# Four scatters issued at the end of the routing, and two products of the first unit made on VectorE

## The reference

```
xn = layernorm(x)
s  = mamba(xn)             # two directions, each with 16 states:
       dt = softplus(x_dbl[..., :64] @ Wdt.T + bdt)
       dBu = dt * B[n] * x ;  deltaA = exp(dt * A[n])        # n = 0..15
       carry = deltaA_t * carry + dBu_t ;  y += carry * C[n]
g  = silu(moe(xn))         # 8 experts, each token goes to its best 2
x  = x + s * g
```

```
x = x + linear_attention_and_mlp(layernorm(x)) * silu(lowrank(layernorm(x)))
```

## Time and profile before

| what | value |
|---|---|
| time, median of 3 runs | 3098.73 us (3096.38 to 3099.82) |
| the profiled execution | 3098.88 us, span of its instructions 3097.0 us |
| busy over the span | PE 83%, DVE 73%, ACT 57%, POOL 56% |
| GpSimd's products L1037 | 256, mean 4534 ns |
| GpSimd's scatters L984 | 64, busy 63.0 us |
| VectorE's scans L1167 | 512, mean 2277 ns |
| VectorE waited for GpSimd's products | 45.5 us, 26 times, longest 7.8 us |

### The profile page before, as it was taken

The page is one execution under the profiler, slowest core; times in us unless marked ns, Lnnn a source line. Parts: engine busy times, 40 slices in busy tenths (PEclk is TensorE's granted clock), DMA queues, the critical chain, the costliest instruction groups (busy, mean ns, idle before and its releaser), DMA issues. The chain is left out here.

```text
span 3097.0 us, 36581 instructions
## 1 busy us (share of the span) xinstructions
PE 2569.9 (83%) x13286; PEld 1693.4 (55%) x13286; DVE 2255.7 (73%) x2797; ACT 1777.0 (57%) x2734; POOL 1733.8 (56%) x567
## 2 busy tenths in 40 slices
PE   5457788788788798788787787678999999999999
PEld 2233655655565565565565565555555556455554
DVE  8689899899999999999999999964244243342430
ACT  4456587688687677777867867522232232332322
POOL 2899788788888879879978978831010010110000
PEclk9668899899899899899999999887999999999999
DMA  7222343334333324333333333341010010110000
GB/s 267 73 74 68 113 142 110 109 122 141 114 120 116 131 97 148 111 110 116 131 125 122 113 116 129 116 152 42 1 34 24 10 34 0 34 34 0 7 7 7
DMA packets 143590, 272.65 MB, mean 88 GB/s; under 512 B 23031, under 2 KB 94174, under 8 KB 142430
## 3 DMA queue, kind: packets, MB, share of 16 engines
q1 hardware_dynamic: 137310, 254.12, 24.2%
q0 software_dynamic: 6144, 16.79, 1.6%
HBM read 230.75 MB, written 40.11 MB: 87 GB/s over the span
## 5 line engine op out<-in xcount | busy, mean ns | idle before, releaser
L1037 POOL TENSOR_TENSOR hs<-u,bb 128x2048 f32<-128x2048 f32 x256 | 1159.2, 4534 | 237.7 <-PE hT L1255 231.7
L1167 DVE TENSOR_TENSOR_SCAN hs<-dA,hs 128x1024 f32<-128x1024 f32 x512 | 1162.7, 2277 | 88.2 <-POOL hs L1037 45.5
L1255 PE MATMUL hT<-ident,hs 128*128 128x128 f32 x3648 | 576.2, 299 | 358.4 <-DVE held L1179 307.5
L1083 ACT ACTIVATE dA<-dt,cols 128x511 f32<-128x511 f32 x1024 | 661.0, 680 | 299.3 <-DVE hs L1167 294.2
L1255 PEld LDWEIGHTS hT<-ident,hs 128*128 128x128 f32 x3648 | 441.9, 152 | 512.8 <-DVE held L1179 207.0
L1179 DVE SCALAR_TENSOR_TENSOR held<-hT,ct,held 128x512 f32<-128x512 f32 x880 | 609.7, 733 | 26.5 <-PE hT L1255 26.0
L1526 ACT ACTIVATE gl<-bank,cols_sb 128x512 f32<-128x512 f32 x192 | 130.6, 687 | 527.4 <-PE bank L1765 527.2
L1765 PE MATMUL bank<-mT,cms_sb 128*128 128x512 f32 x768 | 362.7, 597 | 10.1 <-ACT mT L1520 8.6
L144 POOL COPY cur<-slot 128x8 uint32 (+1 forms) x8 | 1.5, 188 | 640.1 <-DVE held L156 628.4
L1274 PEld LDWEIGHTS moe<-xgT,held 128*128 128x128 f32 x2272 | 293.0, 207 | 53.7 <-issue 27.7
L1274 PE MATMUL moe<-xgT,held 128*128 128x128 f32 x2272 | 306.2, 292 | 12.3 <-ACT xgT L1098 12.0
(11 more groups left out here) (228 smaller groups left out, 3248.7 us busy)
## 6 DMA issues: line engine op xcount, KB each, us to landing
held<-wl SPq DMA_DIRECT2D x71, 1024.0 KB
bb<-b_scratch SPq DMA_DIRECT2D x128, 512.0 KB, 5.1
held<-wl SPq DMA_DIRECT2D x71, 512.0 KB
xg<-xg_scratch SPq DMA_DIRECT2D x71, 128.0 KB
yg_scratch<-yg SPq DMA_DIRECT2D x71, 128.0 KB, 1.7
held<-x SPq DMA_DIRECT2D x16, 512.0 KB, 6.4
xg_scratch<-zero SPq DMA_DIRECT2D x8, 1024.0 KB, 6.8
cb<-b_scratch SPq DMA_DIRECT2D x28, 256.0 KB, 5.8
```

The lines of the kernel that those rows point to most:

```text
L1037: nc.gpsimd.tensor_tensor(hs[n % HS][:, :, :], u[d][:, :, :], row, ALU.mult).then_inc(dBu_ready, 1)
L1083: last = nc.scalar.activation(dst, src, ACT.Exp, scale=cols[:, at:at + 1])
L1167: nc.vector.tensor_tensor_scan(h, decay, h, 0.0, ALU.mult, ALU.add).then_inc(scan_done, 1)
L1255: last = nc.tensor.transpose(hT[c % 2][:, k * P:(k + 1) * P], hs[n % HS][:, k, c * P:(c + 1) * P], ident[:, :])
```

## The change

Two things change. First, two of the eight early chunks (`ROUTED`), four scatters, are issued by GpSimd inside the routing block, behind its last work there, once `slot` is written and the zeros have landed. Behind states 0 and 1 there are still three chunks each, and behind state 2 none. Second, in the first unit VectorE makes the products of states 1 and 2 (`BY_VECTOR`), each immediately ahead of the state's first scan. GpSimd only waits for it (`v_mul`) and raises `dBu_ready`.

```diff
@@ -221,6 +221,8 @@
         placed, zeroed, grouped = sem("placed"), sem("zeroed"), [sem("grouped_early"), sem("grouped_late")]
         EARLY = 8
 
+        ROUTED = 2
+
         OPEN = 3
         GROUPED = 11
         ZERO = 2048
@@ -243,6 +245,12 @@
         b_stored, bb_in = sem("b_stored"), [sem("bb_in0"), sem("bb_in1")]
         a_chain, sp_done, dt_sum, u_ready = sem("a_chain"), sem("sp_done"), sem("dt_sum"), sem("u_ready")
 
+        def group(c, done):
+            for k in range(2):
+                nc.gpsimd.indirect_dma_start(
+                    out=xg_dram, out_offset=bass.IndirectOffsetOnAxis(slot[:, k, c:c + 1], 0),
+                    in_=xa[:, c, :], in_offset=None).then_inc(done, 16)
+
 
 
         POOLN = (2, 9)
@@ -252,6 +260,8 @@
         N_ADD = 2 * NP + 1
         SKIP_AT = 7
 
+
+        BY_VECTOR = (1, 2)
         BEHIND, TURNED = (1, 2, 3, 4), (0, 1, 2, 3)
 
         def turned(unit, n):
@@ -571,6 +581,11 @@
                 for k in range(DB):
                     shifted(k)
                 diagonals(1)
+                pool.wait_ge(taps_ready, 8)
+                pool.wait_ge(placed, 1)
+                pool.wait_ge(zeroed, 16 * N_ZERO)
+                for c in range(TC - EARLY, TC - EARLY + ROUTED):
+                    group(c, grouped[0])
 
             @blockR.scalar
             def _(act):
@@ -858,6 +873,7 @@
             prep = ps("prep", [P, 512], lay0)
 
             setup_g = sem("setup_g")
+            v_mul = sem("vector_products")
             dA_ready, dBu_ready, scan_done = sem("dA_ready"), sem("dBu_ready"), sem("scan_done")
             hT_ready, hT_used, yb_ps = sem("hT_ready"), sem("hT_used"), sem("yb_ps")
             cb_in, p_mul, p_add, skip_ready = sem("c_rows_in"), sem("pool_weighed"), sem("pool_added"), sem("skip_ready")
@@ -978,18 +994,10 @@
             def _(pool):
                 nc.gpsimd.memset(one_row[:, :], 1.0).then_inc(setup_g, 1)
 
-                def group(c, done):
-
-                    for k in range(2):
-                        nc.gpsimd.indirect_dma_start(
-                            out=xg_dram, out_offset=bass.IndirectOffsetOnAxis(slot[:, k, c:c + 1], 0),
-                            in_=xa[:, c, :], in_offset=None).then_inc(done, 16)
-
-
                 def groups(unit, n):
 
                     if unit_is_first(unit):
-                        return range(TC - EARLY, TC)[3 * n:3 * n + 3] if n < OPEN else (n - OPEN,)
+                        return range(TC - EARLY + ROUTED, TC)[3 * n:3 * n + 3] if n < OPEN else (n - OPEN,)
                     return (NS - OPEN + n,) if unit_is_first(unit - 1) and NS - OPEN + n < TC - EARLY else ()
 
                 def adds(d, b, k):
@@ -1033,6 +1041,10 @@
                         pool.wait_ge(hT_ready, NC * (turned(unit, n - HS) + 1))
                     elif later(unit):
                         pool.wait_ge(hT_ready, NC * (turned(unit - 1, n + NS - HS) + 1))
+                    if unit_is_first(unit) and n in BY_VECTOR:
+                        pool.wait_ge(v_mul, BY_VECTOR.index(n) + 1)
+                        pool.sem_inc(dBu_ready, 1)
+                        return
                     row = bb[n // 2 % 2][:, n % 2:n % 2 + 1, :].broadcast_to([P, DB, L])
                     nc.gpsimd.tensor_tensor(hs[n % HS][:, :, :], u[d][:, :, :], row, ALU.mult).then_inc(dBu_ready, 1)
 
@@ -1154,9 +1166,20 @@
                     nc.vector.memset(dA[j][:, :, 0:1], 0.0).then_inc(scan_done, 1)
                     dve.sem_inc(hT_used, 1)
 
+                def product(n):
+                    dve.wait_ge(u_ready, 2)
+                    dve.wait_ge(bb_in[n // 2 % 2], 16 * (n // 4 + 1))
+                    if n >= HS:
+                        dve.wait_ge(hT_ready, NC * (turned(0, n - HS) + 1))
+                    row = bb[n // 2 % 2][:, n % 2:n % 2 + 1, :].broadcast_to([P, DB, L])
+                    nc.vector.tensor_tensor(hs[n % HS][:, :, :], u[0][:, :, :], row, ALU.mult).then_inc(v_mul, 1)
+
                 def scan(d, unit, n, j):
 
                     step = NS * unit + n
+                    if j == 0 and unit_is_first(unit) and n in BY_VECTOR:
+                        product(n)
+                        dve.wait_ge(v_mul, BY_VECTOR.index(n) + 1)
                     dve.wait_ge(dA_ready, 2 * step + j + 1)
                     if j == 0:
                         dve.wait_ge(dBu_ready, step + 1)
```

## The result

The changed kernel takes 3090.88 us (median of 9 runs, 3086.49 to 3093.14), the kernel before on the same chips 3099.29 us (9 runs, 3096.38 to 3100.33). The ratio is 0.9974, with a 95% interval of 0.9965 to 0.9983: it is 8.4 us faster, where 13.3 were forecast. The profiled execution took 3089.19 us, its span is 3087.2 us.

A forecast was written before the change was run, and what follows sets the result against it. GpSimd was taken to pace the stretch from 78.79 us to near 294 us. 14.0 us off its list less TensorE waits of 0.3 and 0.4 gave 13.3 us gained: 3085.6 us (3085.4 against the median), range 3082 to 3090.5.

The forecast's parts named there:

- Cost 0, hidden under VectorE's four `soft` instructions.: Routing block: four scatters run 71.7 to 77.0 us, 1.2 us short of VectorE's end, so they add nothing.
- my 5.3 us for four scatters: Routing block: expected GpSimd time of the four moved scatters, at 1.25 us each with the first 1.21 busy.
- The rival of the block's end: Routing block ends 2 to 5 us later through landing or doubled scatter cost; gain 8 to 11 us; chance 0.06.
- So I take the products and the scatters to run side by side.: Behind the barrier: VectorE's two-SBUF-input products and GpSimd's scatters were taken not to hold each other.
- the pair at 2765.14 us: Late in the earlier profile: two-SBUF-input VectorE work and an indirect transfer, both of usual length, cited against exclusion.
- my rival: States 1 and 2: VectorE and GpSimd exclude each other for a whole scatter run; gain 9.1 us, 3089.8; chance 0.05.
- The 14.0 us that leave GpSimd's list: GpSimd between states 0 and 3: two products and four scatters removed, so state 3 begins at 98.6 us.
- The landing of 1.5 us ahead of the first weigh: Before VectorE's first weigh: the last early scatter lands 1.53 us after issue, by 100.2 us, before the weigh at 103.1.
- 2.7 short of GpSimd: From state 4 to the first later wait: GpSimd keeps 13.7 us gained and VectorE 11.0, a difference of 2.7.
- TensorE's 0.3 and 0.4 us: GpSimd's expected waits for TensorE: 0.3 us at state 4, 0.4 at state 9; as larger hold, rival chance 0.12.
- my 2.34 us of slack: State 9 at 154.60 us: TensorE has turned its buffer by 152.26, 2.34 ahead, the tightest place in between.
- I take the first: GpSimd's count for VectorE's scans: raised only when scatters ahead are done; the alternative starts scans up to 0.9 us earlier.

The follow-up runs named there:

- the kernel with three: Against the changed kernel: VectorE also makes state 0's product (from SBUF), rows of states 1 and 2 read from PSUM; 3083.31 us, ratio 0.9958.
- the products alone: Against the changed kernel: no scatters in the routing block (ROUTED 0), only the two products on VectorE; 3091.08 us, ratio 0.9983 to the kernel before.
- the products from PSUM: Against the changed kernel: ScalarE copies B rows of states 1 and 2 to PSUM, VectorE's products read them there; 3086.61 us, ratio 0.9962.
- the kernel in which GpSimd is kept busy: Against the changed kernel: memsets of the zero tile replace the routing block's scatters, all 16 early scatters behind the barrier; 3094.41 us, one run.

## Why the prediction was wrong

It failed at two steps, both ahead of state 3, each of which had been written down as a rival and given 0.05 or 0.06.

- *"Cost 0, hidden under VectorE's four `soft` instructions."* It cost 2.5 us. I held the end of the last issue (77.0) against VectorE's end (78.24), and left the landing out of this term. The rival's paragraph adds it (1.53 us, 78.5) and calls that no move, because it compares with the end of the block and not with VectorE's end, behind which the barrier needs another 0.36. That is worth 0.4 us (77.0 + 1.90 against 78.52, where GpSimd went on before). The other 2.1 are in the end of the issue: 7.46 us behind the slots (70.93 to 78.39), forecast 5.36 (71.64 to 77.0). Two holds of 0.57 and 1.0 us are in it, and a start 0.86 us behind the slots, where I had 0.06; my 5.3 us for four scatters gave 0.3 back, with a gap behind the last one. The block's end follows 1.90 us behind. The rival of the block's end had it right, in the lower part of its 2 to 5 us.
- *"So I take the products and the scatters to run side by side."* They exclude each other if the scatter starts second: 3.1 us lost. I drew it from the pair at 2765.14 us, where both start at the same instant. What counts is what runs at the start of the scatter: in the changed kernel the scatter at 89.07 is 0.96 us long though a product starts 0.48 us into it, and the next, at 90.33, is held. A pair that starts together can't tell the two cases apart. By the rule of the Trainium skill that I had cited ("SBUF — State Buffer", "Who interferes with whom") the later one is blocked until the other finishes, and the traces agree: the held scatters end 0.82 and 0.83 us behind the product. They agree in this order alone, and for scatters, to which I had carried the rule over. In the other order, product second, nobody is blocked: the product at 89.55 starts within a scatter that runs to 90.03, and takes 2.27 us, no more than the product of state 0 in the kernel with three, which starts beside no scatter (2.29 us). So my rival made too much of it, in letting a run of scatters hold VectorE as a whole.

The two rivals were priced one at a time, at 8 to 11 us and 9.1 us gained. Both came, each in part, and how long the holds are depends on where in a product a scatter happens to start: 1.35 and 1.77 us here, 1.11 and 1.74 with the products alone.

What held:

- The 14.0 us that leave GpSimd's list, and that it is the bound: every experiment moved with its list. With the products alone state 3 begins 6.0 us earlier; 9.0 less the two holds there (1.11 and 1.74) is 6.2.
- The products' length, 2.27 us against 2.4, and no wait of GpSimd for either.
- The landing of 1.5 us ahead of the first weigh: from the end of the last early scatter's issue to the weigh, 103.28 to 104.80.
- VectorE's time is GpSimd's time at the waits of 208.29 and 268.84 us (8.5 to 8.6 us ahead of before, counted from the slots), and nothing behind them takes any back. It had nothing to regain, though: its first weigh was 8.6 us ahead already (33.9 us behind the slots against 42.5), where the forecast had it 2.7 short of GpSimd.

TensorE's 0.3 and 0.4 us didn't come, since they hang on GpSimd being 2.7 us further ahead than VectorE, and it wasn't: VectorE waited for the landing. With the products from PSUM it was ahead (11.7 us gained at state 3, VectorE's first weigh 10.2), and 0.52 us came at state 9. As that is 1.5 us ahead and not 2.7, my 2.34 us of slack there was too much, and that 0.52 lies near my 0.4 is luck. The open question of when the count is raised has an answer: VectorE's scan of state 1 starts at 92.00, 0.18 behind its own product, while the sixth scatter ahead of the count in GpSimd's list starts only at 92.95. At the second count three scatters are still to come: the scan of state 2 starts at 98.82, and they start at 99.79, 101.05 and 102.32. The count doesn't wait for the scatters, and the choice that I made in the prediction ("I take the first") was the wrong one.

## What to carry to other kernels

When work moves beside another engine, look for a pair of rows in which the moved instruction *starts within* the other's, and for both orders; a pair that starts at the same time shows nothing. A transfer issued ahead of a barrier holds it until it has landed, here to 1.90 us behind the end of the last issue, so compare that sum with the other engines' end, and the end of the issue with the holds in it. And an operand in PSUM, copied there by an idle engine, takes a VectorE instruction off GpSimd's way at no cost in its own length.

## What the runs showed of the hardware that I had not expected

- An indirect transfer issued by GpSimd is held by a VectorE `tensor_tensor` with both inputs in SBUF, if it starts within it (0.96 us became up to 2.78), and isn't if one input is in PSUM (0.96), at the same length of the VectorE instruction (2.27 and 2.26 us).
- A scatter didn't hold VectorE. From the slots to the end of VectorE's last instruction in the block it is 6.60 us before and 6.61 in the changed kernel. Beside the memsets of the kernel in which GpSimd is kept busy it is 6.89: a `tensor_scalar` (128x71) takes 0.50 us there in place of 0.20.
- A record can be longer without costing its engine anything. The `tensor_scalar` on `cols` (128x128) took 0.23 us before, 0.39 in the changed kernel, and 1.86 beside the memsets, but the next instruction starts 0.14 or 0.15 us behind its start in all three. Two rows of VectorE's timeline, in the kernel in which GpSimd is kept busy:

```profile
72.76 1.86 DVE L777 TENSOR_SCALAR cols<-cols 128x128 f32<-128x128 f32 x1
72.91 2.35 DVE L333 TENSOR_TENSOR dt<-dt,u 128x1024 f32<-128x1024 f32 x2
```

- A `sem_inc` in GpSimd's list, behind a wait, took effect before scatters that stand ahead of it had started (one at 92.0 against 92.95 us, the next at 98.8, three scatters early).
